# P times V with V stationary in four column tiles, and the inverse row sums brought to the transposed side by TensorE

## The chip, the cores and the metric

One core of one Trainium2 chip. The metric is the device time of one execution in microseconds (us); the kernel before takes 2803.57 us, the median of 3 runs (2802.69 to 2804.83).

## What is computed

128 graphs of 128 tokens with 384 features. Layer L0 is a masked graph attention of two layers; layer L1 is a 12-head attention (head size 32) with the adjacency as bias. The part that the change touches is L1:

```python
scores = jnp.einsum('bqhd,bkhd->bhqk', q, k) * scale + bias
row_nonzero = jnp.any(scores != 0, axis=-1, keepdims=True)
scores = jnp.where(row_nonzero, scores, -jnp.inf)
p = jax.nn.softmax(scores, axis=-1)
p = jnp.nan_to_num(p)
out = jnp.einsum('bhqk,bkhd->bqhd', p, v).reshape(b, n, h)
return out @ Wo.T + bo
```

The result is x = layernorm(x + L0(x)), then layernorm(x + L1(x)).

## The kernel before, in words

The work goes in groups of 4 graphs, 32 groups. A pass of the loop (`passes`, line 249) does L0 of group `it` and L1 of group `it - 1`, interleaved; the first passes and the last ones leave parts out, and the last graph's output stages (`TAIL`) fall into the following pass. Each engine has a `body(p)`: a list, written out by hand, of calls in the order in which that engine issues them (PE from line 1421, DVE 1076, ACT 667, POOL 469). Engines meet only at semaphores. PSUM has 8 banks of 512 floats; `BANK_USES` (line 163) lists for each bank the stages that use it in one pass, in order, and before a stage writes to a bank PE waits until the previous user in that list has been read (`await_bank`).

Float32 precision is had by splitting: an operand is rounded to f16 by ACT (`hi`, line 533, the instruction is line 522), the rest is computed by DVE (`lo`, line 791, instruction line 801 or 803) or POOL, and each product is three matmuls hi\*hi, hi\*lo, lo\*hi.

L1 of one graph b:

- `scores` (PE, line 1362): q times k for 12 heads in three calls. Stationary and moving operands have 32 rows, so the four heads of a call lie in four row tiles. 36 matmuls of 128 columns a graph. DVE's `scores` (line 819) adds the bias, negates and takes the row maximum with `accum_out` (a second instruction, a read of the accumulator).
- `exps` (ACT, line 570): 12 activations of 128 by 128 a graph, in calls of three, into the one buffer `w`; each call waits for PE's transposes of the previous graph's `w`.
- `pt` (PE, line 1379): three calls of four transposes of `w` a graph; ACT rounds to `pT_hi`, DVE makes `pT_lo`.
- `folds` (POOL) and `live_of` (DVE, line 849) find rows whose scores are all zero.
- `pv` (PE, line 1388): for each of 12 heads three matmuls, P transposed (128 by 128) stationary, v with a column of ones (33 columns) moving. The 33rd column gives the row sum.
- `rs_of` (DVE, line 859): reciprocal of the sums out of PSUM, times the live flag. `pv` (DVE, line 870): PSUM times these, into `o`.
- `to` (PE, line 1403): three transposes of `o`; ACT rounds the result (`oT_hi`, line 522), DVE makes `oT_lo` (line 801).
- `po` (PE, line 1412): the output projection; DVE `po` and `po_stats`, ACT `fin`, SP `store` finish.

The other stages that the steps name: `nl` (L0 node products, 512 columns), `hl` (L0 values), `u` (L0 scores, stationary operands 64 columns wide in two column tiles, moving 192 columns, 36 matmuls a call), `ctx` (L0 attention times values), `th`, `x1t` (four transposes a call), `qk`, `v`, `exp_u`, `round_e`, `weigh`, `e_rest` (L0 exponentials and their split), `resid`, `y_bn`, `resid_norm` (the first layernorm).

Of the kernel before, what the change touches and what calls it, by code (L numbers as in the profile page):

```python
# [5 lines left out]
GROUP = 4  # L6
# [6 lines left out]
VCOL = HEAD + 1  # L13
# [19 lines left out]
def program(nc, x, xT, adj, adjT, adjM, weights, biases, ln_cols, ln_rows, out):  # L33
# [5 lines left out]
    with ExitStack() as stack:  # L39
# [46 lines left out]
        v_raw = sb("v_raw", [GROUP, FEAT])  # L86
        v_hi, v_lo = (sb(f"v_{p}", [GROUP, HEADS, VCOL], f16) for p in ("hi", "lo"))
# [3 lines left out]
        nmax, total, live, rs = ([sb(f"{n}{i}", [HEADS]) for i in range(2)] for n in ("nmax", "total", "live", "rs"))  # L91
        pT_hi, pT_lo = ([sb(f"pT{i}_{p}", [HEADS, TOK], f16) for i in range(2)] for p in ("hi", "lo"))
        o = [sb(f"o{i}", [HEADS, HEAD]) for i in range(2)]
# [9 lines left out]
        def signal(name, per_group):  # L103
# [12 lines left out]
            for p in ("u_full", "u_read", "u_sum", "e_raw", "e_ok", "e_hi_ok", "e_lo_ok"))  # L116
# [20 lines left out]
        to_full, to_hi, to_lo = (signal(f"to_{p}", GROUP) for p in ("full", "hi", "lo"))  # L137
# [12 lines left out]
                     rs_ok, mv_ok[1], var_ok[1], pow_ok[1], eps_ok[1], rstd_ok[1], o_ok, to_full, to_hi, to_lo,  # L150
# [6 lines left out]
                "pt": pt_lo, "pv": o_ok, "to": to_lo, "po": y2_ok}  # L157

        def uses(*runs):
# [3 lines left out]
            uses(("nl0", 0), ("x1t", 2), ("v", 0, 2), ("nl1", 1), ("pt", 3), ("pv", 1), ("hl1", 1)),  # L163
            uses(("to", 3), ("hl0", 1, 3), ("qk", 1, 5), ("v", 1), ("pt", 0), ("nl1", 2), ("hl1", 0), ("pt", 7),
                 ("pv", 2), ("po", 1), ("c1", 0)),
            uses(("po", 3), ("qk", 0, 2), ("th", 2), ("v", 3), ("pt", 1), ("pv", 0), ("to", 0), ("nl1", 5),
                 ("to", 2), ("c1", 1)),
            uses(("nl0", 3), ("u0", 0), ("x1t", 0), ("c0", 2), ("qk", 3), ("th", 1), ("nl1", 0, 3), ("pt", 6),
                 ("hl1", 2), ("pt", 11), ("c1", 2)),
            uses(("nl0", 2), ("hl0", 2), ("c0", 3), ("th", 0), ("s", 0, 4), ("pt", 2), ("s", 8), ("po", 0),  # L170
                 ("s", 12), ("u1", 0), ("pt", 9), ("po", 2), ("c1", 3)),
            uses(("nl0", 1, 4), ("u0", 1), ("c0", 0), ("qk", 4), ("s", 1, 5, 9), ("pt", 4), ("s", 13), ("pt", 8),
                 ("hl1", 3)),
            uses(("nl0", 5), ("c0", 1), ("s", 2, 6, 10), ("nl1", 4), ("s", 14), ("to", 1), ("u1", 1)),
            uses(("pv", 3), ("hl0", 0), ("x1t", 1), ("s", 3, 7, 11), ("pt", 5), ("s", 15), ("pt", 10)))

        TAIL = (("pv", 3), ("to", 3), ("po", 3), ("fin", 2), ("fin", 3), ("y2_power", 3), ("store", 3))
        L1_STAGES = ("x1t", "qk", "v", "s", "pt", "pv", "to", "po")
# [156 lines left out]
        def _(pool):  # L335
# [9 lines left out]
            nc.gpsimd.memset(v_hi[:, :, :, HEAD:VCOL], 1.0).then_inc(ones_ok, 1)  # L345
            nc.gpsimd.memset(v_lo[:, :, :, HEAD:VCOL], 0.0).then_inc(ones_ok, 1)
# [9 lines left out]
            pool.wait_ge(ones_ok, 7)  # L356
# [104 lines left out]

            def y2_power(run, b):
                p = run.of("y2_power", b)
                if p is None:
                    return
                pool.wait_ge(y2var_ok.sem, p.upto(y2var_ok, b + 1))
                power(rstd2[:, b % 2:b % 2 + 1], var2[:, b % 2:b % 2 + 1], 1, y2pow_ok)

            def body(p):
                z_power(p, 1)  # L470
                y_power(p)
                hl(p, 0, 0)
                hl(p, 0, 1)
                weigh(p, 0, 0)
                weigh(p, 0, 1)
                e_rest(p, 0, 0)
                e_rest(p, 0, 1)
                hl(p, 0, 2)
                hl(p, 0, 3)
                out_bias(p, 0)  # L480
                out_bias(p, 1)
                y2_power(p, 3)
                scale_adj(p)
                out_bias(p, 2)
                z_power(p, 0)
                folds(p, 0)
                v(p, 0)
                v(p, 1)
                folds(p, 1)
                xt(p, 0)  # L490
                v(p, 2)
                out_bias(p, 3)
# [3 lines left out]
                v(p, 3)  # L496
                xt(p, 2)
                hl(p, 1, 0)
                folds(p, 3)
                hl(p, 1, 1)  # L500
                hl(p, 1, 2)
                weigh(p, 1, 0)
                weigh(p, 1, 1)
                e_rest(p, 1, 0)
                e_rest(p, 1, 1)
                hl(p, 1, 3)
                mask_of(p)
                y2_power(p, 1)
# [11 lines left out]
        def _(act):  # L520
# [43 lines left out]
            def v(p, b):  # L564
                if p.l1:
                    act.wait_ge(v_sum.sem, p.upto(v_sum, b + 1))
                    copy(v_hi[:, b, :, 0:HEAD], v_raw[:, b].rearrange("p (h d) -> p h d", h=HEADS))\
                        .then_inc(vr_hi.sem, 1)

            def exps(p, b, j):  # L570
# [60 lines left out]

            def to(run, b):
                p = run.of("to", b)
# [6 lines left out]
                hi(p, to_full, b, "to", oT_hi[b % 2][:], to_hi)  # L640
# [26 lines left out]
            def body(p):  # L667
                nl(p, 0, 0)
                nl(p, 0, 1)
                nl(p, 0, 2)  # L670
                setup(p, 2)
                setup(p, 3)
                nl(p, 0, 3)
                to(p, 3)
                nl(p, 0, 4)
                nl(p, 0, 5)
                setup(p, 4)
                x1_norm(p, 2)
                x1_norm(p, 3)
                hl(p, 0, 0)  # L680
                hl(p, 0, 1)
                exp_u(p, 0, 0)
                x1t(p, 0)
                x1t(p, 1)
                x1t(p, 2)
                exp_u(p, 0, 1)
                round_e(p, 0, 0)
                round_e(p, 0, 1)
                hl(p, 0, 2)
                hl(p, 0, 3)  # L690
                fin(p, 2)
                qk(p, 0)
                qk(p, 1)
                ctx(p, 0, 0)
                setup(p, 5)
                ctx(p, 0, 1)
# [3 lines left out]
                setup(p, 6)  # L700
                setup(p, 7)
# [6 lines left out]
                v(p, 0)  # L708
# [3 lines left out]
                v(p, 1)  # L712
                v(p, 2)
                exps(p, 0, 3)
                pt(p, 0, 0)
                pt(p, 0, 1)
                pt(p, 0, 2)
                exps(p, 1, 0)
                nl(p, 1, 0)
                exps(p, 1, 1)  # L720
                nl(p, 1, 1)
                xt(p, 0)
                exps(p, 1, 2)
                xt(p, 1)
                nl(p, 1, 2)
                to(p, 0)
                exps(p, 1, 3)
                nl(p, 1, 3)
                pt(p, 1, 0)
                setup(p, 8)  # L730
                exps(p, 2, 0)
                pt(p, 1, 1)
                nl(p, 1, 4)
                pt(p, 1, 2)
                exps(p, 2, 1)
                xt(p, 2)
                exps(p, 2, 2)
                nl(p, 1, 5)
                fin(p, 3)
                pt(p, 2, 0)  # L740
                v(p, 3)
                exps(p, 2, 3)
                setup(p, 9)
                exps(p, 3, 0)
                hl(p, 1, 0)
                pt(p, 2, 1)
                exps(p, 3, 1)
# [32 lines left out]
        def _(dve):  # L780
# [38 lines left out]
            def scores(p, b, j):  # L819
# [5 lines left out]
                if b >= 2:  # L825
                    if j == 0:
                        p.await_apart(dve, fold1, b - 1)
                    p.await_apart(dve, p_ok, (b - 2) * TILES + j + 1)
                elif p.before.l1:
                    if j == 0:  # L830
                        p.before.await_apart(dve, fold1, b + 3)
# [17 lines left out]
            def live_of(p, b):  # L849

                if not p.l1:
                    return
                dve.wait_ge(fold3.sem, p.upto(fold3, b + 1))
# [695 lines left out]
```

## Time and profile before

| | |
|---|---|
| median of 3 runs | 2803.57 us |
| the profiled execution | 2804.14 us |
| its span, first to last instruction | 2802.3 us |
| PE busy | 2748.0 us, 98% |
| DVE busy | 2340.3 us, 84% |
| ACT busy | 1852.7 us, 66% |
| POOL busy | 1475.3 us, 53% |
| granted TensorE clock, mean | 0.990 of full |

PE is the engine of the matmuls, PEld its weight loads, DVE, ACT and POOL the vector, scalar and GpSimd engines. "Busy" is the union of an engine's instructions in time; "mean ns" is the duration of one, and where instructions overlap on one engine busy time divided by count is less than it. "Idle before" is what an engine stood still before a group, with who released it.

### The profile page before, as it was taken

The page shows a single profiled execution, that of the slowest core. Times are in us where ns is not written, and L with a number is a line of the kernel's source. Part 1 is how long each engine was busy: PE and PEld are TensorE (multiplying, and loading weights), DVE is VectorE, ACT ScalarE, POOL GpSimd, SP SyncE. Part 2 cuts the span into 40 slices and gives each one's busy share as a digit, 9 for nine tenths or more (in the row PEclk, how much of TensorE's full clock was granted, in tenths as well). Part 3 has the DMA queues.
Part 4 walks back from the last instruction along what each step waited for, and adds up shares of the span by engine and source line. Part 5 has one row for each costly group of instructions (what it writes and reads, how often), then busy time and mean ns, then how long its engine had stood idle before and what let it go on. Part 6 is the DMA issues. An engine that isn't in the chain of part 4 may idle for free.

```text
span 2802.3 us, 74130 instructions
## 1 busy us (share of the span) xinstructions
PE 2748.0 (98%) x27072; PEld 1758.9 (63%) x27072; DVE 2340.3 (84%) x8170; ACT 1852.7 (66%) x4363; POOL 1475.3 (53%) x1558
## 2 busy tenths in 40 slices
PE   7999999999999999999999999999999999999986
PEld 3566666666666666666666666666666666666654
DVE  4788888888888888888888888888888888888886
ACT  4666676666676666766666766667766667666664
POOL 2555565455555455655455644555555546545543
PEclk9999999999999999999999999999999999999997
DMA  4011011010111110110111110101101101111000
GB/s 169 22 34 49 22 46 46 35 48 22 49 46 35 45 48 21 49 46 32 48 35 35 46 46 34 48 22 48 46 31 49 48 22 48 43 35 48 24 25 22
DMA packets 55992, 116.68 MB, mean 42 GB/s; under 512 B 4944, under 2 KB 37712, under 8 KB 55632
## 3 DMA queue, kind: packets, MB, share of 16 engines
q1 hardware_dynamic: 55632, 111.96, 11.6%
q8 instruction: 217, 3.56, 0.5%
q14 instruction: 143, 1.17, 0.1%
HBM read 86.77 MB, written 25.17 MB: 40 GB/s over the span
## 4 chain that ended last, share of the span: by engine, by line
PE 97%; DVE 1%; issue 1%; ACT 1%; DMA 0%; POOL 0%; SPq 0%; POOLq 0%; DVEq 0%; ACTq 0%
PE psum L1242 72%; PE psum L1252 11%; PE psum L1306 7%; PE psum L1400 4%; PE psum L1374 3%; DMA s<-weights 0%; ACT w L582 0%; DVE pT_lo L801 0%; DVE y L899 0%; POOL sd L427 0%; DVE st L961 0%; DVE s L836 0%; ACT w_hi L522 0%; ACT pT_hi L522 0%; DVE st L907 0%
## 5 line engine op out<-in xcount | busy, mean ns | idle before, releaser
L458 POOL TENSOR_TENSOR fold<-s 128x768 f32<-128x768 f32 x128 | 242.7, 1896 | 505.2 <-DVE nmax L836 432.3
L582 ACT ACTIVATE w<-s,nmax 128x128 f32<-128x128 f32 x1536 | 493.3, 399 | 2.0 <-DVE nmax L836 1.8
L1242 PE MATMUL psum<-hT_hi,w_hi 128*128 128x512 f16 x1152 | 438.8, 381 | 13.1 <-POOL hT_lo L377 11.9
L1242 PE MATMUL psum<-hT_lo,w_hi 128*128 128x512 f16 x1152 | 438.5, 381 | 0.0
L1242 PE MATMUL psum<-hT_hi,w_lo 128*128 128x512 f16 x1152 | 438.5, 381 | 0.0
L522 ACT ACTIVATE nT_hi<-psum 128x512 f16<-128x512 f32 x384 | 227.7, 593 | 305.3 <-PE psum L1242 305.3
L836 DVE CUSTOM_DVE_ANT_0 s<-psum,adj 128x128 f32<-128x128 f32 x1536 | 341.8, 285 | 20.3 <-PE psum L1374 18.0
L385 POOL TENSOR_TENSOR hl_lo<-hl_raw,hl_hi 128x384 fp32r<-128x384 f32 x256 | 242.6, 958 | 138.6 <-ACT hl_hi L522 137.6
L801 DVE TENSOR_TENSOR pT_lo<-psum,pT_hi 128x512 f16<-128x512 f32 x384 | 260.0, 685 | 55.6 <-ACT pT_hi L522 51.7
L522 ACT ACTIVATE pT_hi<-psum 128x512 f16<-128x512 f32 x384 | 223.4, 591 | 100.8 <-PE psum L1252 100.8
L803 DVE SCALAR_TENSOR_TENSOR nT_lo<-psum,nT_hi 128x512 f16<-128x512 f32 x384 | 254.5, 683 | 22.9 <-ACT nT_hi L522 19.6
L427 POOL TENSOR_TENSOR yrstd<-yvar,pw 128x4 f32<-128x4 f32 x32 | 32.4, 1012 | 420.3 <-DVE yvar L988 420.3
L1242 PE MATMUL psum<-w_hi,hT_hi 128*128 128x384 f16 x768 | 251.1, 327 | 0.0
L1242 PE MATMUL psum<-w_lo,hT_hi 128*128 128x384 f16 x768 | 250.4, 326 | 0.0
L1242 PE MATMUL psum<-w_hi,hT_lo 128*128 128x384 f16 x768 | 250.4, 326 | 0.0
L458 POOL TENSOR_TENSOR fold<-fold 128x384 f32<-128x384 f32 (+1 forms) x256 | 218.7, 854 | 20.1
L1252 PE MATMUL psum<-ident,w 128*128 128x128 f32 x1536 | 218.5, 279 | 2.8 <-DVE nmax L836 2.3
L1242 PE MATMUL psum<-xT_hi,w_hi 128*128 128x512 f16 x576 | 219.2, 381 | 0.0
L1242 PE MATMUL psum<-xT_lo,w_hi 128*128 128x512 f16 x576 | 218.8, 380 | 0.0
L1242 PE MATMUL psum<-xT_hi,w_lo 128*128 128x512 f16 x576 | 218.8, 380 | 0.0
L522 ACT ACTIVATE qk_hi<-psum 128x512 f16<-128x512 f32 x192 | 113.9, 593 | 150.3 <-PE psum L1242 150.3
L522 ACT ACTIVATE z<-psum,rden 128x384 f32<-128x384 f32 x256 | 134.5, 577 | 113.5 <-DVE rden L954 113.5
(135 smaller groups left out, 7941.0 us busy)
## 6 DMA issues: line engine op xcount, KB each, us to landing
xTin<-xT SPq DMA_DIRECT2D x32, 768.0 KB, 4.7
xres<-x SPq DMA_DIRECT2D x32, 768.0 KB, 4.6
out<-y SPq DMA_DIRECT2D x128, 192.0 KB, 1.9
adjm<-adjM SPq DMA_DIRECT2D x32, 384.0 KB, 5.3
adjT_sb<-adjT SPq DMA_DIRECT2D x32, 256.0 KB, 5.5
adj<-adj SPq DMA_DIRECT2D x32, 256.0 KB, 2.8
x<-weights SPq DMA_DIRECT2D x4, 576.0 KB, 5.5
s<-weights SPq DMA_DIRECT2D x3, 576.0 KB, 6.4
```

Source lines behind the costliest of these rows:

```text
L385: nc.gpsimd.tensor_tensor(hl_lo[:, b, 0:FEAT], hl_raw[:, b], hl_hi[:, b, 0:FEAT].bitcast(f32), ALU.subtract).then_inc(hlr_lo[l].sem, 1)
L458: nc.gpsimd.tensor_tensor(fold[:, :, 0:n], src[:, :, 0:n], src[:, :, n:2 * n], ALU.add)\
L522: return nc.scalar.activation(dst, src, ACT.Copy, scale=scale)
L582: last = nc.scalar.activation(w[:, m], s[b % 2][:, m], ACT.Exp, bias=nmax[b % 2][:, m:m + 1], scale=-1.0)
L801: nc.vector.tensor_tensor(dst, src, rounded, ALU.subtract).then_inc(done.sem, 1)
L803: nc.vector.scalar_tensor_tensor(dst, src, scale, rounded, ALU.mult, ALU.subtract)\
L836: last = nc.vector.tensor_tensor_reduce(out=s[b % 2][:, m], in0=psum[:, SC[j], c * TOK:(c + 1) * TOK], in1=adj2[:, b], scale=-1.0 / TEMPER ...
L1242: last = mm(dst, a, b, start=(i == 0), stop=(i == total - 1))
L1252: last = transpose(dst[:, n * 128:(n + 1) * 128], src, ident[:])
L1306: last = mm(dst[own], a[:, own], m[:, HALF * j:HALF * j + TRI], start=(n == 0), stop=(n == 3 * KB - 1))
L1374: last = mm(psum[:, SC[j], c * TOK:(c + 1) * TOK], a[rows, 0, c, b], m[rows, 1, c, b], start=(i == 0), stop=(i == 2))
L1400: last = mm(dst[:, n * VCOL:(n + 1) * VCOL], a, m, start=(i == 0), stop=(i == 2))
```

## The change

On PE `pv` has its operands exchanged: v's 32 columns of a head are stationary, P transposed (128 columns) moves, and the four heads of a block of 128 features write to four groups of 32 PSUM partitions. The result is already transposed. So `to` on PE is gone; in its place `rt` transposes the inverse row sums, spread over 32 columns a head. The sums come from `accum_out` of ACT's exponentials; v loses its column of ones.

```diff
 # PE
-                for n in range(HEADS):
-                    h = TILES * (n % KB) + n // KB
-                    terms = split(pT_hi[b % 2][:, n], pT_lo[b % 2][:, n], v_hi[:, b, h], v_lo[:, b, h])
-                    for i, (a, m) in enumerate(terms):
-                        last = mm(dst[:, n * VCOL:(n + 1) * VCOL], a, m, start=(i == 0), stop=(i == 2))
+                for c in range(KB):
+                    for i in range(3):
+                        a, m = ((v_hi, pT_hi), (v_lo, pT_hi), (v_hi, pT_lo))[i]
+                        for j in range(TILES):
+                            d = slice(HEAD * j, HEAD * (j + 1))
+                            last = mm(dst[d, c * TOK:(c + 1) * TOK], a[:, b, c * 128 + HEAD * j:c * 128 + HEAD * (j + 1)],
+                                      m[b % 2][:, KB * j + c], start=(i == 0), stop=(i == 2))
-            def to(run, b):
+            def rt(run, b):
...
+                pe.wait_ge(rs_ok.sem, p.upto(rs_ok, b + 1))
+                run.await_bank(pe, "rt", b)
+                turn("rt", b, [rs[b % 2][:, c].rearrange("p j d -> p (j d)") for c in range(KB)], rt_full)
 # ACT
+                if b >= 2:
+                    act.wait_ge(rcp_ok.sem, p.upto(rcp_ok, b - 1))
...
-                                                scale=-1.0)
+                                                scale=-1.0, accum_out=sums[b % 2][:, m:m + 1])
+            def rt(run, b):
...
+                copy(o[b % 2][:].rearrange("p k t -> p (k t)"), bank("rt", b)[:, 0:FEAT]).then_inc(rt_ok.sem, 1)
             def to(run, b):
...
-                hi(p, to_full, b, "to", oT_hi[b % 2][:], to_hi)
+                act.wait_ge(o_ok.sem, p.upto(o_ok, b + 1))
+                copy(oT_hi[b % 2][:], o[b % 2][:]).then_inc(to_hi.sem, 1)
 # DVE
             def rs_of(run, b):
...
+                dve.wait_ge(p_ok.sem, p.upto(p_ok, (b + 1) * TILES))
+                nc.vector.reciprocal(rcp[b % 2][:], sums[b % 2][:]).then_inc(rcp_ok.sem, 1)
...
+                wide = rcp[b % 2][:].rearrange("p (j c) -> p c j", j=TILES)[:, :, :, None]
+                nc.vector.tensor_copy(rs[b % 2][:], wide.to_broadcast([128, KB, TILES, HEAD])).then_inc(rs_ok.sem, 1)
             def pv(run, b):
...
+                dve.wait_ge(pv_full.sem, p.upto(pv_full, b + 1))
+                dve.wait_ge(rt_ok.sem, p.upto(rt_ok, b + 1))
+                nc.vector.tensor_tensor(o[b % 2][:].rearrange("p k t -> p (k t)"), bank("pv", b)[:, 0:FEAT],
+                                        o[b % 2][:].rearrange("p k t -> p (k t)"), ALU.mult).then_inc(o_ok.sem, 1)
-            def to(run, b):
-                p = run.of("to", b)
-                if p is not None:
-                    lo(p, to_hi, b, "to", oT_lo[b % 2][:], oT_hi[b % 2][:], to_lo)
 # POOL
+            def to(run, b):
...
+                nc.gpsimd.tensor_tensor(oT_lo[b % 2][:], o[b % 2][:], oT_hi[b % 2][:], ALU.subtract)\
+                    .then_inc(to_lo.sem, 1)
```

`v_raw` has two buffers in place of four, with a wait on `vr_lo`; DVE's `scores` waits for `live_ok` in place of `fold1`. All four bodies and `BANK_USES` are written anew. PE's second half of a pass, from the first scores on, is now: scores 0; v 0, 1, 2; scores 1; v 3; pt 0.0, 0.1; nl 1.0, 1.1; pt 0.2; nl 1.2; rt 0; pv 0; scores 2; pt 1.0; nl 1.3; pt 1.1, 1.2; nl 1.4; po 0; nl 1.5; hl 1.0; rt 1; pv 1; scores 3; pt 2.0, 2.1, 2.2; hl 1.1; u 1.0, 1.1; pv 2; hl 1.2; rt 2; po 1; hl 1.3; pt 3.0, 3.1, 3.2; po 2; ctx 1.0 to 1.3. The first half is: nl 0.0, 0.1, 0.2; pv 3; rt 3; nl 0.3, 0.4, 0.5; po 3; hl 0.0, 0.1; u 0.0, 0.1; hl 0.2; x1t 0, 1, 2; hl 0.3; qk 0; ctx 0.0, 0.1; qk 1; ctx 0.2, 0.3; qk 2 to 5; th 0, 1, 2.

ACT's list from the first exponential on is now: exps 0.0 to 0.3; v 0; exps 1.0; pt 0.0, 0.1; exps 1.1; v 1; pt 0.2; nl 1.0, 1.1; exps 1.2; nl 1.2; rt 0; exps 1.3; to 0; pt 1.0; xt 1, 2; nl 1.3; pt 1.1; fin 3; pt 1.2; exps 2.0; nl 1.4; exps 2.1; v 2, 3; nl 1.5; exps 2.2; rt 1; exps 2.3; to 1; hl 1.0; pt 2.0; exps 3.0; pt 2.1, 2.2; exps 3.1, 3.2; hl 1.1; exps 3.3; rt 2; exp_u 1.0, 1.1; to 2; fin 0; hl 1.2; round_e 1.0; pt 3.0, 3.1; round_e 1.1; pt 3.2; hl 1.3; ctx 1.0 to 1.3.

## Rows read from the trace of the kernel before

**Rows 1.** The page: busy time by engine.
```profile
PE 2748.0 (98%) x27072; PEld 1758.9 (63%) x27072; DVE 2340.3 (84%) x8170; ACT 1852.7 (66%) x4363; POOL 1475.3 (53%) x1558
```

**Rows 2.** The waits of PE: line, released by, us in total, times, longest.
```profile
PE psum L1242 <- POOL hT_lo L377: 11.9, 1, 11.9
...
PE psum L1242 <- POOL hl_lo L385: 0.3, 1, 0.3
```

**Rows 3.** The chain that ended last, 1044 to 1140: start us, us, what.
```profile
1052.67 1.46 PE psum L1242 x9
...
1054.57 0.61 PE psum L1374 x36
...
1065.64 0.90 PE psum L1400 x36
...
1069.58 1.94 PE psum L1242 x9
...
1081.70 1.61 PE psum L1306 x36
...
1085.80 0.33 PE psum L1252 x3
...
1137.19 0.87 PE psum L1252 x8
1138.07 1.46 PE psum L1242 x9
```

**Rows 4.** PE's weight loads by line and form: busy us, mean ns.
```profile
L1306 PEld LDWEIGHTS psum<-nT_hi,hT_lo 128*64 128x64 f16 x1536 | 87.1, 110 | 0.0
```

**Rows 5.** ACT by line and form, the exponentials: busy us, mean ns, idle before.
```profile
L582 ACT ACTIVATE w<-s,nmax 128x128 f32<-128x128 f32 x1536 | 493.3, 399 | 2.0 <-DVE nmax L836 1.8 <-issue 0.2
```

**Rows 6.** DVE's timeline, two accumulating operations: start us, us.
```profile
1055.57 0.28 DVE L836 CUSTOM_DVE_ANT_0 s<-psum,adj 128x128 f32<-128x128 f32 x1
1055.78 0.08 DVE L836 DVE_READ_ACCUMULATOR2_ANT nmax<- 128x1 f32 x1
1055.78 0.29 DVE L836 CUSTOM_DVE_ANT_0 s<-psum,adj 128x128 f32<-128x128 f32 x1
```

**Rows 7.** ACT's timeline, second half of a pass: start us, us of the group together.
```profile
1053.65 0.79 ACT L629 ACTIVATE h_raw<-psum,lncol 128x512 f32<-128x512 f32 x1
1054.32 0.79 ACT L629 ACTIVATE hT_hi<-psum,lncol 128x512 f16<-128x512 f32 x1
...
1056.72 2.75 ACT L582 ACTIVATE w<-s,nmax 128x128 f32<-128x128 f32 x9
1059.35 0.95 ACT L522 ACTIVATE v_hi<-v_raw 128x384 f16<-128x384 f32 x2
...
1078.71 0.70 ACT L647 ACTIVATE y<-y,nmr,rstd 128x384 f32<-128x384 f32 x1
1079.31 0.58 ACT L522 ACTIVATE pT_hi<-psum 128x512 f16<-128x512 f32 x1
1079.79 0.52 ACT L522 ACTIVATE v_hi<-v_raw 128x384 f16<-128x384 f32 x1
1080.20 1.90 ACT L582 ACTIVATE w<-s,nmax 128x128 f32<-128x128 f32 x6
...
1092.40 1.90 ACT L593 ACTIVATE e<-uLR 64x256 f32<-64x256 f32 x6
1094.33 0.42 ACT L522 ACTIVATE e_hi<-e 128x256 fp32r<-128x256 f32 x1
1094.65 0.58 ACT L522 ACTIVATE pT_hi<-psum 128x512 f16<-128x512 f32 x1
```

**Rows 8.** PE's timeline, the L0 ctx calls of layer 1: start us, us.
```profile
1096.01 0.47 PE L1242 MATMUL psum<-hl_hi,e_hi 128*128 128x386 f32 x1
...
1098.51 0.39 PE L1242 MATMUL psum<-hT_hi,w_hi 128*128 128x512 f16 x1
```

**Rows 9.** POOL by line and form, a subtraction of 384 columns.
```profile
L393 POOL TENSOR_TENSOR v_lo<-v_raw,v_hi 128x384 f16<-128x384 f32 x128 | 112.7, 892 | 0.0
```

More of the change, by code:

```diff
@@ L90, in program @@
         fold = sb("fold", [HEADS, TOK // 2])
-        nmax, total, live, rs = ([sb(f"{n}{i}", [HEADS]) for i in range(2)] for n in ("nmax", "total", "live", "rs"))
+        nmax, total, live, sums, rcp = (
+            [sb(f"{n}{i}", [HEADS]) for i in range(2)] for n in ("nmax", "total", "live", "sums", "rcp"))
         pT_hi, pT_lo = ([sb(f"pT{i}_{p}", [HEADS, TOK], f16) for i in range(2)] for p in ("hi", "lo"))
-        o = [sb(f"o{i}", [HEADS, HEAD]) for i in range(2)]
+        rs = [sb(f"rs{i}", [KB, TILES, HEAD]) for i in range(2)]
+        o = [sb(f"o{i}", [KB, TOK]) for i in range(2)]
         oT_hi, oT_lo = ([sb(f"oT{i}_{p}", [KB, TOK], f16) for i in range(2)] for p in ("hi", "lo"))
@@ L136, in program @@
             signal(p, GROUP) for p in ("pv_full", "live_ok", "rcp_ok", "rs_ok", "o_ok"))
-        to_full, to_hi, to_lo = (signal(f"to_{p}", GROUP) for p in ("full", "hi", "lo"))
+        rt_full, rt_ok, gate_ok, to_hi, to_lo = (
+            signal(p, GROUP) for p in ("rt_full", "rt_ok", "gate_ok", "to_hi", "to_lo"))
         po_full, y2_ok, y2st_ok, y2mv_ok, y2var_ok, y2pow_ok, y2nmr_ok, fin_ok = (
@@ L177, in program @@
-        TAIL = (("pv", 3), ("to", 3), ("po", 3), ("fin", 2), ("fin", 3), ("y2_power", 3), ("store", 3))
-        L1_STAGES = ("x1t", "qk", "v", "s", "pt", "pv", "to", "po")
+            uses(("pv", 3), ("nl0", 5), ("x1t", 1), ("qk", 2), ("th", 1), ("v", 2), ("pv", 0), ("nl1", 4),
+                 ("hl1", 0), ("pt", 6, 11)),
+            uses(("nl0", 1), ("th", 0), ("v", 1), ("pt", 0), ("nl1", 2), ("pt", 4), ("pv", 1), ("pt", 7)),
+            uses(("hl0", 0), ("x1t", 0), ("c0", 0, 2), ("qk", 5), ("v", 0), ("pt", 1), ("rt", 0), ("nl1", 3),
+                 ("pt", 8), ("hl1", 2), ("pt", 10)),
@@ new lines, in program @@
+            uses(("nl0", 2), ("hl0", 2), ("c0", 1, 3), ("th", 2), ("v", 3), ("pt", 3), ("rt", 1), ("hl1", 1),
+                 ("rt", 2), ("pt", 9), ("c1", 0)),
+            uses(("rt", 3), ("nl0", 4), ("hl0", 1, 3), ("s", 0, 4), ("nl1", 0), ("s", 8), ("pt", 5), ("s", 12),
+                 ("u1", 0), ("c1", 1)),
+            uses(("x1t", 2), ("qk", 3), ("s", 1, 5), ("nl1", 1), ("s", 9, 13), ("po", 1), ("c1", 2)),
+            uses(("po", 3), ("u0", 0), ("qk", 1, 4), ("s", 2, 6), ("pt", 2), ("s", 10), ("po", 0), ("s", 14),
+                 ("pv", 2), ("c1", 3)),
@@ L180, in place @@
+            uses(("nl0", 0, 3), ("u0", 1), ("qk", 0), ("s", 3, 7, 11), ("nl1", 5), ("s", 15), ("u1", 1), ("hl1", 3),
+                 ("po", 2)))
+        TAIL = (("rs", 3), ("rt", 3), ("pv", 3), ("po", 3), ("fin", 2), ("fin", 3), ("y2_power", 3), ("store", 3))
+        L1_STAGES = ("x1t", "qk", "v", "s", "pt", "pv", "rt", "po")
         def place(stage, i):
@@ L460, in folds @@
                     src = fold[:]
+            def to(run, b):
+                p = run.of("pv", b)
+                if p is None:
+                    return
+                pool.wait_ge(to_hi.sem, p.upto(to_hi, b + 1))
+                nc.gpsimd.tensor_tensor(oT_lo[b % 2][:], o[b % 2][:], oT_hi[b % 2][:], ALU.subtract)\
+                    .then_inc(to_lo.sem, 1)
             def y2_power(run, b):
@@ L630, in th @@
                         .then_inc(done.sem, 1)
+            def rt(run, b):
+                p = run.of("rt", b)
+                if p is None:
+                    return
+                act.wait_ge(rt_full.sem, p.upto(rt_full, b + 1))
+                if b >= 2:
+                    act.wait_ge(to_lo.sem, p.upto(to_lo, b - 1))
+                elif p.before.l1:
+                    act.wait_ge(to_lo.sem, p.before.upto(to_lo, b + 3))
+                copy(o[b % 2][:].rearrange("p k t -> p (k t)"), bank("rt", b)[:, 0:FEAT]).then_inc(rt_ok.sem, 1)
             def to(run, b):
-                p = run.of("to", b)
+                p = run.of("pv", b)
                 if p is None:
@@ L685, in body @@
                 x1t(p, 2)
+                fin(p, 2)
+                round_e(p, 0, 0)
                 exp_u(p, 0, 1)
-                round_e(p, 0, 0)
+                hl(p, 0, 2)
                 round_e(p, 0, 1)
-                hl(p, 0, 2)
                 hl(p, 0, 3)
-                fin(p, 2)
+                xt(p, 0)
+                ctx(p, 0, 0)
+                ctx(p, 0, 1)
                 qk(p, 0)
                 qk(p, 1)
-                ctx(p, 0, 0)
-                setup(p, 5)
-                ctx(p, 0, 1)
                 ctx(p, 0, 2)
@@ L724, in body @@
+                nl(p, 1, 2)
+                rt(p, 0)
+                exps(p, 1, 3)
+                to(p, 0)
+                pt(p, 1, 0)
                 xt(p, 1)
-                nl(p, 1, 2)
-                to(p, 0)
-                exps(p, 1, 3)
+                xt(p, 2)
                 nl(p, 1, 3)
-                pt(p, 1, 0)
-                setup(p, 8)
+                pt(p, 1, 1)
+                fin(p, 3)
+                setup(p, 9)
+                pt(p, 1, 2)
                 exps(p, 2, 0)
-                pt(p, 1, 1)
@@ L733, in body @@
                 nl(p, 1, 4)
-                pt(p, 1, 2)
                 exps(p, 2, 1)
-                xt(p, 2)
+                v(p, 2)
+                v(p, 3)
+                nl(p, 1, 5)
                 exps(p, 2, 2)
-                nl(p, 1, 5)
-                fin(p, 3)
+                rt(p, 1)
+                exps(p, 2, 3)
+                to(p, 1)
+                hl(p, 1, 0)
                 pt(p, 2, 0)
-                v(p, 3)
-                exps(p, 2, 3)
-                setup(p, 9)
@@ L759, in body @@
                 exp_u(p, 1, 1)
+                to(p, 2)
+                fin(p, 0)
+                hl(p, 1, 2)
                 round_e(p, 1, 0)
+                pt(p, 3, 0)
+                pt(p, 3, 1)
+                round_e(p, 1, 1)
                 pt(p, 3, 2)
-                round_e(p, 1, 1)
                 hl(p, 1, 3)
@@ L830, in scores @@
                     if j == 0:
[L831 removed]
+                        p.before.await_apart(dve, live_ok, b + 3)
                     p.before.await_apart(dve, p_ok, (b + 2) * TILES + j + 1)
@@ L852, in live_of @@
                     return
+                if b >= 2:
+                    dve.wait_ge(rs_ok.sem, p.upto(rs_ok, b - 1))
+                elif p.before.l1:
+                    dve.wait_ge(rs_ok.sem, p.before.upto(rs_ok, b + 3))
                 dve.wait_ge(fold3.sem, p.upto(fold3, b + 1))
@@ L1061, in v @@
                     return
+                if b >= 2:
+                    dve.wait_ge(vr_lo.sem, p.upto(vr_lo, b - 1))
+                elif p.before.l1:
+                    dve.wait_ge(vr_lo.sem, p.before.upto(vr_lo, b + 3))
                 if p.before.l1:
@@ L1083, in body @@
                 inv_std(p, 1)
[L1084 to L1088 removed]
+                scale_z(p, 1)
                 shift_z(p, 0)
                 shift_z(p, 1)
[L1091 to L1092 removed]
+                pv(p, 3)
                 resid(p, 0)
                 resid(p, 1)
+                nl(p, 0, 2)
+                y_bn(p, 0)
+                y_bn(p, 1)
+                scale_z(p, 2)
                 setup(p, 3)
[L1096 to L1103 removed]
+                setup(p, 4)
+                nl(p, 0, 3)
+                scale_z(p, 3)
+                setup(p, 5)
+                shift_z(p, 2)
+                shift_z(p, 3)
+                nl(p, 0, 4)
+                nl(p, 0, 5)
+                po(p, 3)
+                resid(p, 2)
                 resid(p, 3)
@@ L1149, in body @@
                 scores(p, 0, 2)
+                th(p, 1)
                 scores(p, 0, 3)
-                th(p, 1)
+                th(p, 2)
+                v(p, 0)
                 v(p, 1)
-                v(p, 2)
-                v(p, 3)
-                th(p, 2)
+                setup(p, 7)
                 scores(p, 1, 0)
                 scores(p, 1, 1)
+                scores(p, 1, 2)
+                scores(p, 1, 3)
+                live_of(p, 0)
+                setup(p, 8)
                 pt(p, 0, 0)
                 pt(p, 0, 1)
-                setup(p, 7)
+                rs_of(p, 0)
+                v(p, 2)
                 pt(p, 0, 2)
-                scores(p, 1, 2)
-                live_of(p, 0)
-                rs_of(p, 0)
-                scores(p, 1, 3)
-                fin(p, 3)
-                pv(p, 0)
                 nl(p, 1, 0)
                 nl(p, 1, 1)
+                v(p, 3)
+                nl(p, 1, 2)
+                pv(p, 0)
                 scores(p, 2, 0)
@@ L1219, in body @@
                 den(p, 1, 1)
+                fin(p, 1)
                 bn(p, 1, 0)
@@ L1223, in body @@
                 bn(p, 1, 3)
-                fin(p, 1)
             def head():
```

256 lines of the change are left out of this document (103 added, 153 removed).

## The prediction

> **What bounds the kernel now.** I read the page's busy times first, to see which engine could be the bound: PE is busy 98% of the span, DVE 84%, ACT 66%, POOL 53% [rows 1]. Busy says little by itself, so next the waits of PE: there are twelve kinds, the longest 11.9 us and once, and all of them together are 48 us, at the start and the end of the program [rows 2]. Then the chain that ended last, over one pass: it never leaves PE. From one hl call to the same call of the next pass it takes 1138.07 - 1052.67 = 85.40 us [rows 3], and 32 passes are 2733 of the 2802 us. So time is won only where PE issues less, and lost where ACT, DVE or POOL come later than PE's list asks for them. The chain gives every call of PE a price [rows 3]: scores 0.61 us, nl or qk 1.94, hl, v or po 1.46, one u 1.61, pv 0.90, three transposes (to, rt) 0.33, four (pt, th) 0.44. The four ctx calls take 98.51 - 96.01 = 2.5 us [rows 8].
>
> **PE: pv.** Removed: 36 matmuls a graph with 128 by 128 weights and 33 moving columns, 0.90 us. Added: 36 matmuls with 32-column weights and 128 moving columns, four at a time in four column tiles. Not in the trace. Nearest rows: scores, which has 36 matmuls of 128 moving columns, four at a time in row tiles: 0.61 us, or 17 ns each [rows 3]; u, 36 matmuls of 192 columns, two at a time in column tiles: 1.61 us [rows 3], and 18 steps of 192 columns at the full 2.4 GHz (80 ns) are 1.44, so column tiles do run side by side. From below, nine steps of 53 ns with nothing between are 0.48 us. From above, no gain: a matmul may still cost the 25 ns that 0.90 us for 36 make. I take scores' 0.61: same count, same columns, same four-fold packing. Gain 0.29 us a graph, 1.16 a pass, 128 x 0.29 = 37 us in all; at 0.48 it is 54, at 0.90 nothing.
>
> Here two rules speak against the change. The u rows say that narrow weights in column tiles cost little: their 64-column loads last 110 ns each [rows 4], far more than 1.61 us / 36 = 45 ns, so they overlap. The Trainium skill (TensorEngine Tiling (Array Packing), Restrictions and Gotchas) says that column tiling switches fast weight load off, and TensorE: Matmul & The Clock Gate (Back-to-back issue gap) that start-to-start never falls below about 25 ns; by that floor pv would stay at 36 x 25 = 0.90 us and the gain would be zero. The trace contradicts the floor for row tiles, where scores runs at 17 ns.
>
> **PE: the turn.** Three transposes of `o` go, three of `rs` come, 0.33 us each way: nothing. But rt now needs only the exponentials' sums and the live flags, not pv, and the chain behind pv (DVE's product, ACT's rounding, POOL's rest, then po) must be hidden. In the new list at least nl 0.3 to 0.5 (5.8 us), scores to nl 1.4 (5.8 us), scores 3 to rt 2, or hl 1.2 to pt 3.2 (6.0 us) lie between pv and po, against about 2 us of work (DVE's product, 0.41 on ACT, 0.89 on POOL [rows 7, 9]): hidden.
>
> **DVE and POOL.** DVE gives up `oT_lo` and gets a spreading copy of the same 384 columns: even. Its product waits for rt's copy on ACT, and behind it in DVE's queue stand the next graph's scores, for which ACT's exponentials and then PE's pt wait. On the clock used below PE ends rt 0 at 14.5, so ACT's copy (0.41) can end at 14.9, with the exponentials before it some 1 us later, and PE gives scores 2 only at 15.75: at most tenths, which the tail's charge covers. POOL gets four subtractions of 0.89 us a pass [rows 9], 3.6 us on top of 46; at 53% busy [rows 1] there is room, and I charge nothing. If there were none, it would come to the wait for `e_lo` and `hl_lo` at the end of the pass, where the tail below puts it. SP's queue issues what it did.
>
> **ACT.** It gets four copies of 384 columns a pass (rt) and, with `accum_out`, a read of the accumulator behind each of 48 exponentials. Its price in pitch, call it a, is the unknown. Exponentials last 399 ns [rows 5] but start 292 ns apart (2.63 us for nine [rows 7]). From below a = 0, as on DVE, where the 0.08 us read of the accumulator runs beside the next operation and the pitch stays 0.21 us [rows 6]; a gain is excluded, as ACT does the same and more. From above, ACT may drain before the read: the 107 ns of overlap are lost and 80 ns added, a = 0.187. I take a = 0.08, the read's own length laid end to end: DVE is the only row for this operation, and ACT need not hide it as DVE does.
>
> Now what PE leaves time for. Clock 0 is the start of scores 0. ACT's six th activations, 0.67 us apart [rows 7], begin about 0.5 us after PE's first th call and so end at 3.2; exponentials start there.
> - To pt 2.2 PE issues 4 scores, 4 v, 8 pt, 6 nl, 2 rt, 2 pv, po and hl: 28.2 us. ACT must by then have done 36 exponentials (10.5), 4 v, 3 rt and to at 0.41, 14 of 512 columns at 0.48 and a fin of 0.60 [rows 7]: 3.2 + 10.5 + 1.6 + 1.2 + 6.7 + 0.6 = 23.9. Room 4.3 us, or a up to 0.12.
> - To the last ctx call PE takes 43.3. That call needs ACT's hl 1.3, then POOL (0.89) and a handoff, so ACT must end by 42.3. It has 48 exponentials (14.0), 4 v, 10 of 384 columns, 20 of 512, 2 fin, two exp_u (1.93), two round_e (0.32 each) [rows 7]: 3.2 + 14.0 + 1.6 + 4.1 + 9.6 + 1.2 + 1.9 + 0.6 = 36.3. Room 6.0 us, a up to 0.125.
>
> At a = 0.08 both hold. But rt 2 stands ahead of exp_u in ACT's list: it can't start before 35.8, and what follows to hl 1.3 (rt, exp_u, to, fin, hl, round_e, pt, round_e, pt, hl) is 6.2 us, ending at 42.0 against 42.3. So the tail is tight with any a, and I charge 0.3 us a pass for handoffs there, 32 x 0.3 = 10 us; without them it is 0.
>
> **Sum.** 37 - 10 = 27 us. Against the profiled execution's own time, 2804.1 (span 2802.3 and 1.8 around it), this gives 2777; against the median of the runs, 0.5 us lower, 2776.
>
> **Rivals.**
> - ACT becomes the bound: slower. Place: the exponentials and the tail of the second half. It costs nothing to a = 0.12, and above it PE waits 48 x (a - 0.125) us a pass; it outweighs pv's gain from 48 x (a - 0.125) = 1.16, a = 0.149. At a = 0.187 PE waits 3.0 us, a net loss of 1.8 a pass: 2804 + 32 x 1.8 = about 2862. For it: each ACT operation shows a 107 ns tail that only overlap hides. Against it: DVE's read is hidden whole. 0.27.
> - pv doesn't get faster: the column tiles issue at 25 ns each. 0.90 us stays, the tail's 0.3 us remains charged: 2804 to 2813. For it: u falls short of its ideal by 12%, and four narrow loads at a time are shown nowhere; the rule above. Against it: scores. 0.10.
> - The first half: rs 3 on DVE comes before shift_z, resid and the layernorm that x1t 0 waits for, and DVE is the busiest after PE. If x1t came 0.5 us late in every pass, 16 us of the gain would go: 2792. If it were a full microsecond, 2808. 0.08.
> - The forecast: 0.55, from 2750 (pv at 0.48, no tail) to 2790.
>
> **Numbers.** A measurement tells 0.2% (5.6 us) from no change. Faster: 0.55 for the forecast, and 0.05 of the cases where only part of the gain goes: 0.60. Same: half of "pv stays" and the ACT case near its turning point, 0.10. Slower: the ACT case, half of "pv stays", the late first half: 0.30. The range starts at 2750 and reaches into the ACT case to 2845 (a = 0.175), leaving out about one in ten above. The forecast's own range is 2750 to 2790.
>
> **What would show it.** Right: the chain is still PE; pv pieces of about 0.61 us; a pass of about 84.5 us; exponentials at a pitch under 0.41 us; PE without waits on `w` or `hl_lo` but for tenths at ctx. Wrong: exponentials 0.47 us apart, PE waiting on `w` at pt 2.2 and on `hl_lo` or `e_lo` at ctx, ACT busy over 80%; or pv still at 0.9 us; or x1t waiting on `x`.

## The result

The changed kernel takes 2865.6 us, the median of 4 runs (2855.9 to 2874.2), against 2803.8 for the kernel before: ratio 1.0221, with an interval of 1.0204 to 1.0237. It is slower by 62 us. The forecast was 2776, with a range to 2845; its sign was wrong.

The page of the changed kernel: busy times, then the chain that ended last, by engine and by line.

```profile
span 2862.0 us, 76301 instructions
PE 2739.2 (96%) x27072; PEld 1705.6 (60%) x27072; DVE 2321.3 (81%) x8170; ACT 2020.1 (71%) x6027; POOL 1572.3 (55%) x1684
...
PE 87%; DMA 5%; ACT 3%; DVE 1%; issue 1%; SPq 1%; POOL 0%; DVEq 0%; ACTq 0%; POOLq 0%
PE psum L1273 65%; PE psum L1283 10%; PE psum L1337 7%; DMA xTin<-xT 5%; PE psum L1405 3%; PE psum L1432 3%; ACT xT_hi L533 2%; ACT y L673 1%; ACT z L533 1%; SPq L309 0%; SPq L301 0%; DVE pT_lo L831 0%; DMA s<-weights 0%; DVE s L866 0%; DVE rs L909 0%
```

Against [rows 1], PE went from 98 to 96% busy and ACT from 66 to 71%: ACT is not full. What is new stands in the chain: a transfer, xTin, has 5% of the span, and PE, which never left the chain in a pass before, has 87%. The first of PE's waits (line, released by, us in total, times, longest) says the same, against [rows 2], where no wait came back pass after pass:

```profile
PE psum L1273 <- ACT z L533: 62.7, 30, 3.4
PE psum L1283 <- DVE rs L909: 11.9, 5, 3.4
PE psum L1273 <- POOL hT_lo L378: 11.6, 1, 11.6
```

And what ACT waited for before it rounded x (by line and form: busy us, mean ns, then idle before):

```profile
L533 ACT ACTIVATE hT_hi<-xTin 128x512 f16<-128x512 f32 x96 | 57.0, 634 | 87.2 <-DMA xTin<-xT 87.2
```

The chain of the changed kernel around 1054 (start us, us, what) shows link by link where the time goes:

```profile
1053.90 0.45 PE psum L1283 x4
1054.35 0.02 issue
1054.37 1.58 ACT xT_hi L533 x3
1055.95 0.03 issue
1055.97 0.71 ACT y L673
1056.69 0.02 issue
1056.70 0.33 SPq L301
1057.04 0.04 issue
1057.08 0.43 SPq L309
1057.51 0.05 issue
1057.57 0.02 SPq L313
1057.58 0.03 issue
1057.61 4.72 DMA xTin<-xT
...
1062.36 0.02 ACT hT_hi L533
...
1062.89 0.57 ACT z L533
1063.46 0.14 issue
1063.60 10.75 PE psum L1273 x42
```

Read it downwards. First come x1t (PE) and its rounding on ACT, then fin 2 on ACT (`y`), which finishes the output of graph 2. SP, whose list issues the transfers, has the store of graph 2 (line 301) ahead of the load of `adj` (309) and of the load of xTin for the next group, so xTin is issued at 1057.61, as soon as fin 2 allows it, and takes 4.7 us. The new list of ACT has xt 0, the first call that reads xTin, ahead of ctx 0.0. ACT reaches it at 1059.5 and stands 2.9 us, with the first PSUM result of ctx behind it in its queue; PE waits 2.0 us for the bank that ACT has not read. In the kernel before, the same load was issued behind fin 2 too, but xt 0 stood behind nl 1.1: 25 us from issue to use (SP's and ACT's timelines of the kernel before):

```profile
1041.87 0.40 SPq L311 DMA_DIRECT2D xTin<-xT  x1
```

```profile
1067.04 0.63 ACT L522 ACTIVATE hT_hi<-xTin 128x512 f16<-128x512 f32 x1
```

In some of the passes PE's clock falls on top of the wait. The busy time of each engine in stretches of the same place in two passes (columns: stretch, us, PE, PEld, DVE, ACT, POOL busy with counts, granted clock, DMA share, GB/s):

```profile
1061.70:1063.60 1.90, 0.00 (x0) 0.03 (x1) 0.11 (x1) 1.24 (x3) 1.74 (x3) 1.00 0.71 275
1063.60:1064.80 1.20, 1.20 (x6) 0.97 (x6) 0.92 (x2) 1.20 (x3) 1.20 (x2) 0.90 0.00 0
1064.80:1068.00 3.20, 3.20 (x9) 1.21 (x9) 2.75 (x10) 1.15 (x3) 0.67 (x2) 0.50 0.01 3
1068.00:1070.00 2.00, 2.00 (x11) 0.90 (x10) 0.78 (x6) 0.60 (x1) 1.01 (x1) 1.00 0.01 4
```

```profile
1238.00:1240.00 2.00, 0.01 (x2) 0.04 (x1) 0.12 (x1) 1.25 (x3) 1.84 (x3) 1.00 0.81 315
1240.00:1242.00 2.00, 2.00 (x11) 1.37 (x12) 1.57 (x5) 1.53 (x4) 1.84 (x3) 1.00 0.03 8
```

After the first idle stretch PE runs 3.2 us at 0.50, that is at 1.2 GHz, which costs 1.6 us against the same work at 2.4; after the second, as long as the first, it stays at full clock. The u calls in the chain (three starts of the same call in following passes) give the two kinds of pass, 1281.05 to 1368.95 = 87.90 us with such a fall (granted clock 0.67 from 1326 to 1330) and 1368.95 to 1455.22 = 86.27 us without:

```profile
1281.05 3.09 PE psum L1337 x72
...
1368.95 3.09 PE psum L1337 x72
...
1455.22 3.09 PE psum L1337 x72
```

The terms that the prediction did price are close to it. pv (L1432) takes 0.62 us for 36 matmuls, rt 0.33:

```profile
1002.09 0.33 PE psum L1283 x3
1002.41 0.62 PE psum L1432 x36
1003.03 0.61 PE psum L1405 x36
```

And the exponentials, with a read of the accumulator each (ACT's timeline: start us, us), start 0.385 us apart (the first twelve of a pass, 1078.85 to 1083.47) instead of 0.292 [rows 7]:

```profile
1082.31 0.41 ACT L596 ACTIVATE w<-s,nmax 128x128 f32<-128x128 f32 x1
1082.60 0.21 ACT L596 ACTIVATION_READ_ACCUMULATOR w<-s,nmax 128x1 f32 x1
1082.70 0.41 ACT L596 ACTIVATE w<-s,nmax 128x128 f32<-128x128 f32 x1
1082.99 0.21 ACT L596 ACTIVATION_READ_ACCUMULATOR w<-s,nmax 128x1 f32 x1
```

### The profile page after: what moved, and what is told of

Read it like the earlier page. It is cut to its first block, busy times and chain, and to the rows that moved or that the text cites. A ratio compares the mean times of both kernels' runs of the same rounds, so it can differ in the third digit from the quotient of the medians.

```text
span 2862.0 us, 76301 instructions
## 1 busy us (share of the span) xinstructions
PE 2739.2 (96%) x27072; PEld 1705.6 (60%) x27072; DVE 2321.3 (81%) x8170; ACT 2020.1 (71%) x6027; POOL 1572.3 (55%) x1684
## 4 chain that ended last, share of the span: by engine, by line
PE 87%; DMA 5%; ACT 3%; DVE 1%; issue 1%; SPq 1%; POOL 0%; DVEq 0%; ACTq 0%; POOLq 0%
PE psum L1273 65%; PE psum L1283 10%; PE psum L1337 7%; DMA xTin<-xT 5%; PE psum L1405 3%; PE psum L1432 3%; ACT xT_hi L533 2%; ACT y L673 1%; ACT z L533 1%; SPq L309 0%; SPq L301 0%; DVE pT_lo L831 0%; DMA s<-weights 0%; DVE s L866 0%; DVE rs L909 0%
## 5 line engine op out<-in xcount | busy, mean ns | idle before, releaser
L596 ACT ACTIVATE w<-s,nmax 128x128 f32<-128x128 f32 x1536 | 599.2, 409 | 3.1 <-DVE nmax L866 2.1
L596 ACT ACTIVATION_READ_ACCUMULATOR w<-s,nmax 128x1 f32 x1536 | 320.4, 209 | 0.0
L831 DVE TENSOR_TENSOR pT_lo<-psum,pT_hi 128x512 f16<-128x512 f32 x384 | 248.9, 684 | 61.2 <-ACT pT_hi L533 57.0
L533 ACT ACTIVATE hl_hi<-hl_raw 128x384 fp32r<-128x384 f32 x256 | 131.0, 519 | 157.4 <-DVE hl_raw L846 156.6
L466 POOL TENSOR_TENSOR oT_lo<-o,oT_hi 128x384 f16<-128x384 f32 x128 | 117.4, 917 | 219.1 <-ACT oT_hi L533 218.9
L533 ACT ACTIVATE pT_hi<-psum 128x512 f16<-128x512 f32 x384 | 217.0, 593 | 19.8 <-PE psum L1283 19.8
L1273 PE MATMUL psum<-xT_hi,w_hi 128*128 128x512 f16 x576 | 227.6, 395 | 0.0
L1273 PE MATMUL psum<-xT_lo,w_hi 128*128 128x512 f16 x576 | 226.2, 393 | 0.0
L1273 PE MATMUL psum<-xT_hi,w_lo 128*128 128x512 f16 x576 | 225.0, 391 | 0.0
L992 DVE BATCH_NORM_STATS2 st<-z 128x6 f32<-128x384 f32 x256 | 130.3, 550 | 110.2 <-ACT z L533 106.6
```

The lines of the kernel that those rows point to most:

```text
L466: nc.gpsimd.tensor_tensor(oT_lo[b % 2][:], o[b % 2][:], oT_hi[b % 2][:], ALU.subtract)\
L533: return nc.scalar.activation(dst, src, ACT.Copy, scale=scale)
L831: nc.vector.tensor_tensor(dst, src, rounded, ALU.subtract).then_inc(done.sem, 1)
L992: nc.vector.bn_stats(st[l][:, b], z[:, b]).then_inc(st_ok[l].sem, 1)
L1273: last = mm(dst, a, b, start=(i == 0), stop=(i == total - 1))
```

## The experiments

Theory A: the loss is the place of xt 0 behind the late transfer. Theory B, the rival of the prediction: the loss is ACT's load by the accumulator reads.

**e1, xt 0 moved to a gap of ACT.**

```diff
 # ACT body
                 hl(p, 0, 3)
-                xt(p, 0)
                 ctx(p, 0, 0)
...
                 qk(p, 3)
+                xt(p, 0)
                 qk(p, 4)
 # POOL body
-                xt(p, 0)
                 y2_power(p, 3)
                 z_power(p, 0)
+                xt(p, 0)
                 folds(p, 0)
```

> The changed kernel with one call moved: ACT's xt 0 (first rounding of the next group's x) from before ctx 0.0 to between qk 3 and qk 4, and POOL's xt 0 with it to between z_power and folds 0. Theory A (the loss is ACT's queue standing at xt 0 for the transfer into xTin, which SP issues only behind the store of graph 2 and so behind fin 2): the wait of ACT on the transfer (87 us in the changed kernel) and PE's wait on z (63 us) go, the clock stays at full, a pass falls from about 87 to 84.5 us, and the time is about 2776 us (2765 to 2790), below the kernel before. Theory B (the loss is ACT's load by the accumulator reads): ACT's work is the same, the time stays above 2850.

Measured: 2792.8 us (2790.6 to 2793.3), 0.996 of before with an interval of 0.9945 to 0.9975. Theory B falls: with the same work for ACT, 73 us came back. PE's wait on z is 1.2 us in all. But the time is 17 us above what A expected. The timeline of e1, DVE and POOL, shows why (start us, us):

```profile
1383.30 2.49 DVE L1039 TENSOR_SCALAR z<-z,rstd,nmr 128x384 f32<-128x384 f32 x4
1383.49 1.30 POOL L378 TENSOR_TENSOR hT_lo<-xTin,hT_hi 128x512 f16<-128x512 f32 x1 [0.84 <-ACT hT_hi L533]
...
1385.72 2.47 DVE L833 SCALAR_TENSOR_TENSOR qk_lo<-psum,qk_hi 128x512 f16<-128x512 f32 x4
...
1387.64 0.10 PEld L1405 LDWEIGHTS psum<-qk_hi 32*128 32x128 f16 x4 [0.34 <-DVE qk_lo L833]
```

Four normalisations of z on DVE take 2.49 us, where they take 1.65 in the kernels before and after. The second of them starts at 1383.70 and lasts 1315 ns where one alone lasts 475, and it ends 0.2 us after POOL's subtraction (1383.49 to 1384.79). DVE is late by 0.8 us with qk_lo and PE's scores wait for it; a pass of e1 is 84.67 us, 0.51 more than in e2 below. ACT is not the delay here, for it waits for PE before its next rounding of qk (0.83 us). The Trainium skill (SBUF — State Buffer, Who interferes with whom) says that a DVE `tensor_scalar` may use two ports and then shuts GpSimd out or is shut out for a whole instruction; the trace agrees, with 1315 against 475 ns. In e1 I had put POOL's xt 0 exactly beside them. No run moves POOL's call alone, so the 0.51 us are read from the chain and not tested.

**e2, SP's list alone.** The edits move the store of graph 2 behind the loads of the next pass; ACT's list is the changed kernel's.

```diff
-        TAIL = (..., ("y2_power", 3), ("store", 3))
+        TAIL = (..., ("y2_power", 3), ("store", 2), ("store", 3))
 # SP body
+                store(p, 2)
                 store(p, 3)
...
-                for b in range(3):
+                for b in range(2):
                     store(p, b)
```

> The changed kernel with SP's list alone edited: the store of graph 2 stands behind the transfers of adj2, xTin, adjm and adjT of the next pass in place of ahead of them; ACT's order, xt 0 ahead of ctx 0.0, is untouched. Theory A: xTin is then issued at the pass boundary, some 20 us earlier, and is there when ACT asks for it: about 2776 us (2765 to 2790). If it matters where xt 0 stands in itself (0.5 us of ACT ahead of ctx), up to 2800. Theory B: stays above 2850.

Measured: 2774.8 us (2774.4 to 2775.2), 0.9898 of before (0.9881 to 0.9914): 91 us below the changed kernel and 29 below the kernel before. SP's timeline now has the load ahead of the store, 24 us before ACT asks for it at 1364.80, and ACT's xt 0 follows hl 0.3 at once:

```profile
1340.67 0.41 SPq L314 DMA_DIRECT2D xTin<-xT  x1
...
1362.11 36.27 SPq L301 DMA_DIRECT2D out<-y  x2
```

```profile
1364.39 0.51 ACT L534 ACTIVATE hl_hi<-hl_raw 128x384 fp32r<-128x384 f32 x1
1364.80 0.62 ACT L534 ACTIVATE hT_hi<-xTin 128x512 f16<-128x512 f32 x1
```

A pass is 84.16 us (u calls of the chain, 1239.57 to 1323.73):

```profile
1239.57 3.09 PE psum L1338 x72
...
1323.73 3.09 PE psum L1338 x72
```

**e3, the changed kernel without accumulator reads.**

```diff
-                                                scale=-1.0, accum_out=sums[b % 2][:, m:m + 1])
+                                                scale=-1.0)
 # POOL, once
+            nc.gpsimd.memset(sums[0][:], 1.0).then_inc(ones_ok, 1)
+            nc.gpsimd.memset(sums[1][:], 1.0).then_inc(ones_ok, 1)
```

> The changed kernel without accum_out on the exponentials; the sums are a constant 1, so the softmax isn't normalised. The order of all lists is the changed kernel's. Theory A: the wait for xTin hangs on fin 2 and not on ACT's load; the time stays at 2855 to 2875 us. Theory B: 48 x 0.094 = 4.5 us of ACT a pass are gone, the time falls to 2780 or less.

Measured: 2868.0 us (2862.0 to 2871.6). All 1536 reads are gone and nothing is gained; ACT stood 85.2 us for the transfer, where it stood 87.2 in the changed kernel. The loss doesn't need the reads.

**e4, the kernel before with xt 0 moved alone.**

```diff
 # ACT body (in all passes but the first)
                 fin(p, 2)
+                xt(p, 0)
                 qk(p, 0)
...
                 nl(p, 1, 1)
-                xt(p, 0)
 # POOL body (likewise)
                 out_bias(p, 1)
+                xt(p, 0)
...
                 folds(p, 1)
-                xt(p, 0)
```

> The kernel before with xt 0 alone moved to right behind fin 2 on ACT (about where the changed kernel has it), and POOL's xt 0 to behind out_bias 1; in the very first pass both keep their old place. No accumulator reads, old pv. Theory A: ACT stands for the transfer from about fin 2's end to 5.7 us later (1126.3 to 1132 in the pass of the trace of before), qk 0 is read so late that PE's qk 2 waits some 3 us and loses clock on top: 3 to 4 us a pass, about 2900 to 2930 us. Theory B: ACT has no more work than before, the time stays within 0.3% of 2804.

Measured: 3004.8 us (3003.7 to 3005.1), 1.0717 of before (1.0701 to 1.0733). The sign and the mechanism are theory A's, but the time is outside its range: 201 us are lost where 2900 to 2930 are 96 to 126. ACT stood 5.7 us a pass on the mean (166.7 us, 29 times), as counted, and 5.56 in the pass shown:

```profile
1017.73 0.69 ACT L650 ACTIVATE y<-y,nmr,rstd 128x384 f32<-128x384 f32 x1
1023.98 0.63 ACT L525 ACTIVATE hT_hi<-xTin 128x512 f16<-128x512 f32 x1 [5.56 <-DMA xTin<-xT]
```

PE's part of it was larger than my 3 us, 4.6 us a pass, and the clock took the rest: PE's busy time is 2816.5 us against 2748.0 [rows 1] for the same matmuls, and the 68.5 us more make 201 with the 132.3 of the wait. The waits of PE, then the stretch around one of them, with the granted clock at 0.69:

```profile
PE psum L1248 <- DVE qk_lo L809: 132.3, 29, 5.4
```

```profile
1020.00:1030.00 10.00, 5.63 (x19) 2.64 (x18) 4.06 (x15) 3.77 (x8) 4.93 (x6) 0.69 0.47 169
```

**e5, e2 without the accumulator reads** (edit as in e3, on e2).

> e2 (SP's store 2 behind the loads) without accum_out, sums a constant 1 (the softmax isn't normalised). Asks what the 1536 accumulator reads cost once the transfer is out of the way. Theory A1 (PE is the bound again, ACT has room up to 0.12 us an exponential and the reads take 0.094): the same as e2, 2775 us within 4. Theory B1 (the reads still push ACT behind PE somewhere): at least 10 us less than e2.

Measured: 2775.6 us (2774.5 to 2777.5), e2's time within a microsecond. The reads cost nothing here, though ACT's busy time falls from 2023 to 1895 us.

**e6, the kernel before with e2's SP edit.**

> The kernel before with SP's list edited as in e2. A control: there xTin is used some 20 us after it lands, so by theory A the SP order is worth nothing there, 2803.5 us within 4, and the 29 us by which e2 is below the kernel before come from pv. If SP's order helps by itself, it is faster than that by 6 us or more.

Measured: 2802.9 us (2801.8 to 2805.1), ratio 1.000 (0.999 to 1.0009). SP's order is worth nothing by itself in the kernel before; what e2 wins against the kernel before comes from the change.

**e7, fin 2 on ACT ahead of x1t.**

```diff
+                fin(p, 2)
                 x1t(p, 0)
                 x1t(p, 1)
                 x1t(p, 2)
-                fin(p, 2)
```

> The changed kernel with fin 2 on ACT ahead of the three x1t roundings in place of behind them, all else untouched. The store and the transfer behind it are issued about 1.7 us earlier, and ACT's x1t still fit in its gaps. Theory A: ACT's wait on the transfer falls from 2.9 to about 1.2 us a pass, PE's wait on z from 2.0 to some 0.3, the clock stays at full: 2785 to 2815 us. Without a dependence on the transfer: 2860 or more.

Measured: 2778.5 us (2777.6 to 2780.3), 0.9913 of before (0.9897 to 0.993). With fin 2 some 1.7 us earlier, a move of a single line, 87 of the 91 us are back, more than I expected. ACT still stands 39.8 us for the transfer, but PE's wait on z is down to 4.4 us.

```profile
PE psum L1273 <- ACT z L533: 4.4, 4, 2.4
```

**e8 and e9, more load on ACT in e2.** A further exponential into a scratch tile ahead of each call of `exps` (e8) or, under `if j in (1, 3)`, of every second one (e9); nothing is left out.

```diff
                 act.wait_ge(s_ok.sem, p.upto(s_ok, b * TILES + j + 1))
+                nc.scalar.activation(junk[:, j], s[b % 2][:, KB * j], ACT.Exp, bias=nmax[b % 2][:, KB * j:KB * j + 1],
+                                     scale=-1.0)
```

> e2 with one more 128 by 128 exponential (into a scratch tile that nobody reads) ahead of each call of exps, 16 a pass, 0.292 us each: the added pitch per exponential is then 0.094 + 0.097 = 0.19 us, the upper bound of the prediction. By the prediction's budget (room 0.125) PE waits 48 x 0.066 = 3.2 us a pass, and the time is about 2775 + 100 = 2875 us. If ACT's gaps take it up: under 2785.

Measured: 2864.9 us (2864.0 to 2866.4), 90 above e2 where 100 was expected. Two starts of u give 1398.10 - 1311.04 = 87.06 us a pass, 2.9 more than in e2 where the formula gave 3.2, and the chain runs through ACT's exponentials (`ACT w L600` 15% of the stretch from 1300 to 1400). PE's waits are short and spread: in the steady passes none is over 0.5 us, and they are mostly on `nT_lo`, `o`, `oT_lo` and `w`, while the prediction had put them on `w`, `hl_lo` or `e_lo`. So e8 bears out the price of a full ACT, and its place only in part.

```profile
1311.04 3.09 PE psum L1341 x72
...
1398.10 1.93 PE psum L1341 x43
```

> e2 with half the extra load of e8: the additional exponential ahead of every second call of exps (j = 1 and 3), 8 a pass, 2.3 us. The added pitch per exponential is on the mean 0.094 + 0.049 = 0.143 us, which lies just above the room of 0.125 that the prediction worked out. By its formula PE waits 48 x 0.018 = 0.9 us a pass: 2775 + 28 = 2803 us. If the true room is larger than 0.143, 2775 within 4; if ACT had no room beyond the reads, 8 x 0.292 x 32 = 75 us more, 2850.

Measured: 2796.4 us (2795.4 to 2798.2), 0.9975 of before (0.9964 to 0.9986); 21.6 above e2, 0.7 us a pass where the formula gave 0.9. So ACT's room ends between the reads' own 0.094 us an exponential (e2 against e5: free) and 0.143 (e9: not free), which brackets the 0.12 to 0.125 that the prediction took from two sums.

## Why the prediction was wrong

Step by step, by its own terms:

- **pv**: forecast 0.61 us in column tiles, measured 0.62. The scores row was the right neighbour: 17 ns a matmul. The 25 ns floor of the Trainium skill (TensorE: Matmul & The Clock Gate, Back-to-back issue gap) does not hold for four column tiles: 0.62 us for 36 matmuls is 17 ns each.
- **The accumulator read**: forecast a = 0.08, measured 0.385 - 0.292 = 0.093. Its instruction lasts 0.21 us, not 0.08; most of that runs beside the next exponential. The room of 0.12 that it was held against is bracketed by e5 and e9, and the price above it is borne out by e8, 2.9 against 3.2 us a pass.
- **The turn, DVE and POOL**: PE's waits on rt and on `oT_lo` are confined to the ends of the program; nothing to pay in a steady pass.
- **The tail**: charged 0.3 us a pass. e2's pass is 84.16 us. A pass before is 85.22 by the same measure (u to u, 1371.66 to 1456.88; my 85.40 was from one hl call to the next), so 1.06 came off, where four times 0.28 for pv is 1.12: the tail costs 0.06 us, 2 us in all and not 10.
- **The ends of the program** were put at nothing. From the last u of a first half to the end, e2 takes 2772.6 - 2617.08 = 155.5 us and the kernel before 2802.3 - 2650.37 = 151.9, so 3.6 us are lost there. pv's 36 less 2 and 4 are 30, and e2 gains 29: that it lands within 2 us of the forecast's 2776 is in part luck, as the tail was too dear by 8 and the ends too cheap by 4.
- **The first half** was the rival with the right half of the pass and the wrong wait. It looked for x1t late because of rs 3. x1t was on time.
- **What failed** is the sentence "SP's queue issues what it did". The order of SP's list is indeed untouched, but the change moved xt 0, the first of the three calls that read xTin, from behind nl 1.1 to ahead of ctx 0.0: from some 20 us after its data lands to 3 us before. xt 0 appears nowhere in the prediction's working of the first half; it counted PE's list call by call and ACT's only from the first exponential on. A moved wait was not priced, and the queue behind it (ctx on ACT, the bank on PE) was not followed.

What the missing term is worth: the changed kernel is 2865.6 - 2774.8 = 91 us above e2, which differs in the order of SP alone; the two profiled executions differ by 89. The changed kernel's trace has 29 full passes from one u of a first half to the next. In 14 of them the clock fell to half behind the wait, and they take 88.19 us on the mean; in 15 it did not, and they take 86.38. Against e2's 84.16 that is 14 x 4.03 + 15 x 2.22 = 90 us, the whole difference: 25 us of it (14 x 1.81) are the clock, the rest the wait. PE's busy time gives nearly the same share, 2739.2 against 2709.2 us in e2. The spread of the runs, 2856 to 2874, is much wider than in e2, and their mean granted clock goes the other way from their time (0.984 at 2856, 0.983, 0.981, 0.978 at 2874): the number of passes in which the clock falls can differ from run to run. Why it falls in one pass and not in the next is open.

The rival "ACT becomes the bound" gives nearly the same time, 2862, for another reason. That it agrees is chance, which only the traces and e3 tell: the reads can all be taken out and the loss stays.

## What to carry to other kernels

When an order by hand is rewritten, make a list of the calls that moved, and for each write down what it waits for on other queues, transfers first: when was it issued, behind what does its queue hold it, when does it land, and is that before the call's new place. A call that was harmless 20 us later can hold an in-order engine for a transfer, and everything queued behind it with it. And two theories that give the same time must be told apart by what they would each leave unchanged, here by taking away the accumulator reads.

## What the runs showed of the hardware

- An accumulator read on ACT lasts 209 ns on the mean, but adds 93 ns to the pitch of 128-column exponentials (0.385 against 0.292 us). On DVE the read starts together with the next operation, at a pitch of 0.21 us [rows 6]; no run shows that pitch without it.
- Four column tiles with 32-column weights run 36 matmuls of 128 columns in 0.62 us, as fast as four row tiles (0.61).
- PE's idle stretches of about 2 us between dense work were followed by a stretch at half clock in 14 of 29 passes (3.2 us or more in the one shown) and by no fall in the other 15, with the same work around them; in e7, where most of those stretches are gone, the mean granted clock is back from 0.983 to 0.991.
- Beside a POOL subtraction one of DVE's `tensor_scalar` on SBUF took 1315 instead of 475 ns in the pass shown of e1; a pass is 0.51 us longer than in e2, and the run 18 us.
